# A graph attention layer on one core: groups of 12 tiles for groups of 8, and one-hots turned by a five-row matmul

## The reference

```python
def head(w1, bb1, w2, bb2, a1, aab1, a2, aab2):
    feats = jnp.maximum(x @ w1 + bb1, 0.0) @ w2 + bb2          # (12500, 64)
    x_cat = jnp.concatenate([feats[row], feats[col], elem[:, None]], axis=1)
    hid = jnp.maximum(x_cat @ a1 + aab1, 0.0)                  # (200000, 129)
    e1 = leaky_relu((hid @ a2 + aab2)[:, 0], 0.2)
    w = jnp.exp(e1 - jnp.max(e1))
    pooled = segment_sum(w[:, None] * feats[col], row, n)
    row_sum = segment_sum(w, row, n) + 1e-10
    return pooled / row_sum[:, None]
h = vmap(head)(...)                                            # 4 heads
out = layernorm(x + transpose(h, (1, 0, 2)).reshape(n, -1))
```

## Time and profile before

| | |
|---|---|
| median of 3 runs | 4587.36 us (4585.55 to 4588.11) |
| the profiled execution | 4587.18 us, span 4585.4 us |
| TensorE, busy share of the span | 90% |
| VectorE | 89% |
| ScalarE | 72% |
| GpSimd | 51% |
| tile loop: first to last hidden part | 1316 to 4451 us |

### The profile page before, as it was taken

One profiled execution on the slowest core, in us unless ns is written; L12 is line 12 of the kernel. 1 busy time (PEld: TensorE's weight loads), 2 busy tenths in 40 slices (PEclk: granted clock), 3 DMA queues, 4 the chain that ended last, 5 costly groups with the idle time before them and its releaser, 6 DMA issues.

```text
span 4585.4 us, 128801 instructions
## 1 busy us (share of the span) xinstructions
PE 4132.6 (90%) x25516; PEld 2946.2 (64%) x25517; DVE 4094.2 (89%) x21278; ACT 3319.3 (72%) x11283; POOL 2340.7 (51%) x2495
## 2 busy tenths in 40 slices
PE   2599999999889999999999999999999999999990
PEld 1255555555567777777777777777777777777760
DVE  8888888888779999999999999999999999999988
ACT  1244444444468888888888888888888888888875
POOL 5444444444445555555555555555555555555535
PEclk9799999999989999999999999999999999999995
DMA  2144444444477777777777777777777777777757
GB/s 90 42 99 89 104 96 91 102 96 93 99 220 224 228 223 226 222 224 226 225 224 223 225 227 221 225 225 226 226 220 223 227 226 223 223 226 224 218 157 224
DMA packets 266911, 851.78 MB, mean 186 GB/s; under 512 B 107916, under 2 KB 109584, under 8 KB 266861
## 3 DMA queue, kind: packets, MB, share of 16 engines
q0 software_dynamic: 169920, 673.54, 52.8%
q1 hardware_dynamic: 63543, 160.18, 11.7%
q10 hardware_dynamic: 33398, 17.49, 1.5%
HBM read 739.10 MB, written 111.90 MB: 186 GB/s over the span
## 4 chain that ended last, share of the span: by engine, by line
PE 38%; ACT 28%; issue 3%; DVE 2%; DMA 0%; ACTq 0%; POOL 0%; DVEq 0%; SPq 0%; POOLq 0%
ACT z L1191 19%; PE psum L1003 16%; PE psum L1007 9%; PE psum L990 9%; ACT onehot L1220 4%; ACT onehot_t L1209 3%; PE psum L1016 3%; ACT onehot L1224 2%; PE psum L971 1%; DVE z L1727 1%; DVE z L1720 1%; PE psum L1027 0%; ACT onehot L1222 0%; DVE z L1743 0%; DVE z L1738 0%
## 5 line engine op out<-in xcount | busy, mean ns | idle before, releaser
L761 POOL DMA_INDIRECT z<-qf_table,rec x1664 | 1605.9, 965 | 1458.8 <-PE psum L990 1038.6
L1191 ACT ACTIVATE z<-z 128x64 f32<-128x64 f32 x6656 | 1651.1, 335 | 0.0
L1003 PE MATMUL psum<-p_win,onehot_t 128*128 x9984 | 1409.7, 274 | 87.2 <-ACT onehot_t L1209 67.0
L1003 PEld LDWEIGHTS psum<-p_win,onehot_t 128*128 128x128 bf16 x9984 | 966.5, 97 | 541.6 <-issue 213.0
L990 PE MATMUL psum<-z,onehot 128*128 128x260 f32 x3328 | 1031.9, 392 | 3.8 <-DVE acc L1655 3.5
L1007 PE MATMUL psum<-z,ident 128*128 128x258 f32 x3328 | 1002.2, 383 | 0.0
L1606 DVE SCALAR_TENSOR_TENSOR z<-z,a_b 128x129 f32<-128x129 f32 x3328 | 881.4, 289 | 3.7 <-issue 0.2
L1606 DVE SCALAR_TENSOR_TENSOR z<-psum,a_b 128x129 f32<-128x129 f32 x3328 | 827.5, 286 | 0.0
L721 POOL DMA_INDIRECT sorted_rows<-z x300 | 475.0, 1583 | 635.9 <-DVE z L1484 487.3
L1596 DVE TENSOR_TENSOR z<-z,psum 128x258 f32<-128x258 f32 x1664 | 698.0, 419 | 98.5 <-PE psum L1007 97.2
L1655 DVE TENSOR_TENSOR acc<-acc,psum 125x260 f32 x1664 | 701.5, 422 | 26.2 <-PE psum L990 4.1
(11 more groups left out here) (230 smaller groups left out, 4602.9 us busy)
## 6 DMA issues: line engine op xcount, KB each, us to landing
p_table<-acc SPq DMA_DIRECT2D x100, 338.6 KB
p_win<-p_table SPq DMA_DIRECT2D x100, 338.6 KB
z<-qf_table,rec POOLq DMA_INDIRECT x1664, 4.5
qf_table<-acc SPq DMA_DIRECT2D x75, 339.5 KB
acc<-in_x_dram SPq DMA_DIRECT2D x25, 448.0 KB
z<-in_x_dram SPq DMA_DIRECT2D x20, 560.0 KB
out_dram<-z ACTq DMA_DIRECT2D x20, 560.0 KB
qf_table<-z SPq DMA_DIRECT2D x25, 339.5 KB
```

Source lines behind the costliest of these rows:

```text
L761: pool.indirect_dma_start(out=z_t[:, o + j, :], out_offset=None, in_=qf_table, in_offset=bass.IndirectOffsetOnAxis(ap=rec[:, o + j, 3:4].b ...
L1003: mm = pe.matmul(to, onehot_t[:, j, :], p_flat[:, bass.ds((w % 2) * (3 * ZW) + (part * ZW + o), n)], start=(part == 0), stop=(part == 2 an ...
L1191: op = act.activation(z_t[:, slot, o:o + DO], z_t[:, slot, o:o + DO], ACT.Copy, scale=z_t[:, slot, o + DO:o + HF])
```

## The change

- Groups of 12 tiles (`SB` = 12) in three batches of four, in the same ring of 24 slots, which now holds two groups. The padded number of tiles is 1668, 139 groups.
- `onehot_t` gets 24 slots. Its rows below 125 come from one bf16 matmul for four tiles, of `node_k` (five rows: 2n, -1, -1, and 1-n*n in two parts, for the ramp n) with `edge_k` (five rows: the edge's row r, r*r in two parts, and ones), so that the result is 1-(r-n)^2, and ACT takes it with a Relu. Rows 125 to 127, the parts of the edge's weight, are written by a DMA for a whole group, and so are the first three rows of `edge_k` (`load_edges`, begun a group ahead; both come from a new table `row_feats`).
- `onehot` (edges in partitions) has only 12 slots and is made in the step in which it is used; its rows come from a small load of their own (`load_rows`). Records shrink to two words.
- Sums follow the hidden part by 18 tiles (`LAG` = 6) where it was 16; gathers go to the group ahead as slots come free.
- The record stage writes three tables: ScalarE copies fields, GpSimd squares the rows and splits the squares, SP stores records, rows and features. PE turns three fields and not six.

```diff
-    SB = 8
+    SB = 12
+    BATCH = 4
+    NBATCH = SB // BATCH
+    LAG = 6
     RING = 24
...
-        onehot = sb("onehot", [P, RING, P])
-        onehot_t = sb("onehot_t", [P, SB, P], BF16)
-        rec = sb("rec", [P, RING, 4])
+        onehot = sb("onehot", [P, SB, P])
+        row_e = sb("row_e", [P, RING])
+        onehot_t = sb("onehot_t", [P, RING, P], BF16)
+        rec = sb("rec", [P, RING, 2])
...
@@ PE, turn @@
-                    group = (i * SPB + (k + off)) * 2 + u
-                    pe.wait_ge(s_onehot, group + 1)
-                    since(pe, s_oht, group)
-                    for j in range(HALF_SB):
-                        mm = pe.transpose(psum[:, 6, j * P:(j + 1) * P], onehot[:, ((k + off) * SB + u * HALF_SB + j) % RING, :], ident[:, :])
-                    mm.then_inc(s_oht_mm, 1)
+                    batch, kn = (i * SPB + (k + off)) * NBATCH + u, (k + off) % SPB
+                    if u == 0:
+                        pe.wait_ge(s_edge_k[kn], i * 16 + ((k + off) // SPB + 1) * 16)
+                    since(pe, s_oht, batch)
+                    pe.matmul(psum[0:WN, 6, 0:BATCH * P], node_k[:, 0:WN], edge_k[:, kn, u * BATCH:(u + 1) * BATCH, :].rearrange("p t n -> p (t n)"),
+                              start=True, stop=True).then_inc(s_oht_mm, 1)
...
@@ PE, step @@
-                    if j == SB // 4 and live(i, k, 0):
+                    if j == 0 and live(i, k, 0):
                         turn(0, 1)
...
+                    if j == 4 and live(i, k, 0):
+                        turn(0, 2)
+                    if j == 8 and live(i, k, 1):
                         turn(1, 0)
...
-                    if j < SB - 1 and live(i, k, -2):
-                        sum_up(-2, j)
+                    if j < LAG and live(i, k, -2):
+                        sum_up(-2, j + SB - LAG)
+                    if j >= LAG and live(i, k, -1):
+                        sum_up(-1, j - LAG)
...
@@ ACT @@
+                def load_rows():
+                    kn = k % SPB
+                    act.dma_start(row_e[:, kn * SB:(kn + 1) * SB], edge_rows[:, bass.ds((i * SPB + k) * SB, SB)]).then_inc(s_row_e[kn], 16)
+
+                def load_edges():
+                    kn = (k + 1) % SPB
+                    if live(i, k, -1):
+                        act.wait_ge(s_z_mm, tile(-1, SB - 1) + 2)
+                    act.dma_start(onehot_t[WN:P, kn * SB:(kn + 1) * SB, :],
+                                  row_feats[bass.ds((i * SPB + (k + 1)) * SB, SB), 3:6, :].rearrange("t f n -> f t n")).then_inc(s_edge_w[kn], 16)
+                    act.dma_start(edge_k[0:3, kn, :, :], row_feats[bass.ds((i * SPB + (k + 1)) * SB, SB), 0:3, :].rearrange("t f n -> f t n"))\
+                       .then_inc(s_edge_k[kn], 16)
+
+                if live(i, k, -1):
+                    onehots(0)
+                if live(i, k, 1):
+                    load_edges()
                 if live(i, k, 0):
                     take_turned(0, 1)
-                if live(i, k, 1):
-                    onehots(1, 0)
                 if live(i, k, -1):
                     exps()
-                if live(i, k, 2):
+                if live(i, k, 0):
+                    load_rows()
+                if live(i, k, 1):
                     load_records()
                 for j in range(SB):
                     if live(i, k, -1):
                         weight(j)
-                    if j == 0 and live(i, k, 1):
+                    if j == 3 and live(i, k, -1):
+                        onehots(1)
+                    if j == 4 and live(i, k, 0):
+                        take_turned(0, 2)
+                    if j == 7 and live(i, k, 1):
                         take_turned(1, 0)
-                    if j == SB // 2 and live(i, k, 1):
-                        onehots(1, 1)
+                    if j == 9 and live(i, k, -1):
+                        onehots(2)
```

More of the change, by code:

```diff
@@ L373, in gnn_layer @@
         CR = 5
-        SC = next(NSB // n for n in range(1, NSB) if NSB % n == 0 and NSB // n <= P)
-        KS = NSB // SC
+        SC = next(NSH // n for n in range(1, NSH) if NSH % n == 0 and NSH // n <= P)
+        KS = NSH // SC
         assert CGROUPS * CG == W and CGROUPS % CR == 0
@@ L413, in gnn_layer @@
         N_PARTS = 5
-        N_TAB_STEPS = 13
+        N_TAB_STEPS = 14
+        assert SB == 12 and all(t * 683 >> 13 == t // SB for t in range(NT))
         EMPTY_W = CHUNKS // P * SF
@@ L419, in gnn_layer @@
         N_PICK = EC // CH
[L420 to L421 removed]
+        BULK = NTS // P
         def live(i, k, off):
@@ L694, in _ @@
             pool.wait_ge(s_weights, N_W)
[L695 to L701, removed]
@@ L967, in _ @@
                 pe.wait_ge(s_stage[g % 4], g // 4 * 16 + 16)
-                since(pe, s_field_a, g - 1)
-                since(pe, s_field_b, g - 1)
-                for f in range(NF):
-                    mm = pe.matmul(psum[:, g % 2 * 6 + f // 3, f % 3 * P:(f % 3 + 1) * P],
+                since(pe, s_field_a, 2 * g - 2)
+                for f in range(3):
+                    mm = pe.matmul(psum[:, g % 2 * 6, f * P:(f + 1) * P],
                                    stage[:, g % 4, :].rearrange("p (s f) -> p f s", f=NF)[:, f, :], ident[:, :], start=True, stop=True)
@@ L1203, in take_turned @@
                 def take_turned(off, u):
[L1205 to L1220 removed]
+                    batch, at = (i * SPB + (k + off)) * NBATCH + u, (k + off) % SPB * SB + u * BATCH
@@ new lines, in take_turned, with onehots @@
+                    if live(i, k, off - 2):
+                        act.wait_ge(s_z_mm, tile(off - 2, u * BATCH + BATCH - 1) + 2)
+                    act.wait_ge(s_oht_mm, batch + 1)
+                    act.activation(onehot_t[0:WN, at:at + BATCH, :].rearrange("p t n -> p (t n)"), psum[0:WN, 6, 0:BATCH * P], ACT.Relu).then_inc(s_oht, 1)
+                def onehots(u):
+                    batch, own, kn = (i * SPB + (k - 1)) * NBATCH + u, slice(u * BATCH, (u + 1) * BATCH), (k - 1) % SPB
+                    if u == 0:
+                        act.wait_ge(s_row_e[kn], i * 16 + ((k - 1) // SPB + 1) * 16)
+                    if live(i, k, -2):
+                        act.wait_ge(s_agg, tile(-2, u * BATCH + BATCH - 1) + 1)
+                    for j in range(u * BATCH, (u + 1) * BATCH):
+                        op = act.activation(onehot[:, j, :], iota_row[:, :], ACT.Abs, scale=-1.0, bias=row_e[:, kn * SB + j:kn * SB + j + 1])
@@ L1221, in onehots @@
                     op.then_inc(s_row_dist, 1)
-                    act.activation(onehot[:, oo:oo + HALF_SB, WN:P], rec_b[:, oo:oo + HALF_SB, 2:5], ACT.Copy)
-                    act.wait_ge(s_row_dist, group + 1)
-                    act.activation(onehot[:, oo:oo + HALF_SB, 0:WN], onehot[:, oo:oo + HALF_SB, 0:WN], ACT.Relu, scale=-1.0,
-                                   bias=ones_f[:, 0:1]).then_inc(s_onehot, 1)
+                    act.wait_ge(s_row_dist, batch + 1)
+                    act.activation(onehot[:, own, :], onehot[:, own, :], ACT.Relu, scale=-1.0, bias=ones_f[:, 0:1]).then_inc(s_onehot, 1)
```

272 lines of the change are left out of this document (163 added, 109 removed).

## The result

| | before | after |
|---|---|---|
| median | 4587.4 us (4 runs) | 4969.4 us (4 runs, 4952.6 to 4986.8) |
| ratio, 95% interval | | 1.0834 (1.0795 to 1.0872) |
| the profiled execution | 4587.18 us | 4952.55 us, span 4950.8 us |
| first hidden part of the loop | 1316.4 us | 1312.7 us |
| first matmul of the last stage | 4473.2 us | 4838.4 us |

The change makes the kernel 8.3% slower. The forecast was 4618 us, within 4490 to 4690. The direction was right; the size was not, and the time is outside the range.

What follows compares the result with a forecast made beforehand. A ring of waits through ScalarE's in-order queue was taken as the bound; 4587 us plus 23 (139 groups of 22.75 us against 208 of 15.09), 3 for the record stage and 5 for the drain gave 4618 us, range 4490 to 4690.

Steps and rivals of the forecast that it cites:

- The ring: Chain of waits through ScalarE's in-order queue and TensorE's tile 8, claimed to set a 12-tile group at 22.75 us.
- register loop: Engines going round their loop at the group start, with TensorE starting cold: 0.3 us, an estimate without a row.
- `e_sh` to first scaling: On ScalarE, two exponentials and two exposed DMA issues between `e_sh`'s start and the first scaling: 1.37 us.
- `e_sh` to tile 8: From `e_sh`'s start through ScalarE's scalings, a one-hot batch and the take to TensorE's tile 8: 9.08 us.
- tile 8 to next tile 0: On TensorE, four tiles of 1.535 us and a turn of 0.22: 6.36 us.
- tile 0 to the transpose of maxima: On TensorE, from the next group's tile 0 to its transpose of the maxima: 4.39 us.
- transpose to `e_sh`: From the transpose of the maxima to the start of `e_sh`, which VectorE makes: 2.62 us.
- the turn: TensorE's five-row bf16 matmul of 512 columns replacing four fp32 transposes: 0.22 us, upper bound 0.43.
- rival 3: TensorE's clock halves after the new 2.5 us gap: 4683 us for a quarter of groups, 4891 for all; chance 0.16.
- Rivals 1: ScalarE's DMA issues run before `e_sh` comes, so a group takes 21.88 us: 4497 us in all; chance 0.15.
- Rival 2: No ring in the tile loop, the fullest engine binds: 20.5 us a group, 4306 us in all; chance 0.12.
- Outside the loop: Record stage, 3 us more, and the drain's extra scalings and batches, 5 us more.

Runs made afterwards that it cites:

- experiment 8: Changed kernel with tile 8's wait filled by nine unused products and the turn on 128 rows of constants (one-hots wrong): 4661.9 us, ratio 1.0162 to the kernel before.
- experiment 2: Changed kernel with nine unused 128-column fp32 products on TensorE ahead of tile 8's wait: 4745.9 us, ratio 1.0343 to the kernel before.
- experiment 3: Changed kernel with the DMA issue of the rows' load moved ahead of the exponentials: 4766.9 us, ratio 1.0385 to the kernel before.
- experiment 1: Changed kernel with the third turned batch's take ahead of the second one-hot batch and tile 4's scalings: 4442.5 us, ratio 0.9686 to the kernel before.
- 10: Kernel of experiment 1 with the turn over all 128 rows, right data, nothing left out: 4378.1 us, ratio 0.9544 to the kernel before.

## Why the prediction came out wrong

**The ring was right.** The take on ScalarE behind scalings and a batch of one-hots sets tile 8, TensorE idles there, and the group is no shorter for being rebuilt. Its terms at full clock, the measured ones as means of 20 groups without and 18 with a turn of the register loop:

| from | forecast | measured, no loop turn | measured, with one |
|---|---|---|---|
| `e_sh` to first scaling | 1.37 | 1.37 | 1.37 |
| `e_sh` to tile 8 | 9.08 | 9.11 | 9.11 |
| tile 8 to next tile 0 | 6.36 | 6.91 | 7.46 |
| tile 0 to the transpose of maxima | 4.39 | 4.83 | 4.82 |
| transpose to `e_sh` | 2.62 | 2.49 | 2.60 |
| register loop | 0.3 | 0 | in the terms above |
| sum | 22.75 | 23.33 | 23.99 |

The register loop comes round in every second group, so the mean is 23.66 us (23.64 over the 45 groups), and the loop's share of it, 0.33 us, was forecast well.

**First mis-sized term: the turn, 0.22 for 0.55 us.** I took it from columns alone and gave it an upper bound of 0.43, the price of the four transposes, both of which have 128 rows. There are two in the ring: 0.66 us of the 0.89 us between 22.75 and 23.64, and experiment 8 takes 0.60 of it back. The rest is 0.1 us each at tiles 8 and 0, whose first hidden part takes 0.92 us and not 0.82, another 0.12 ahead of tile 0, and 0.13 less behind the transpose of the maxima. The bound was too low, and the trace of before held a better row than the one I used. It spreads the maxima with a matmul of four rows:

```profile
2705.98 0.60 PE L1007 MATMUL psum<-z,ident 128*128 128x258 f32 x2
2706.51 0.38 PE L1027 MATMUL psum<-max_diag,ones_f 4*128 4x4 f32 x2
2706.82 0.71 PE L990 MATMUL psum<-z,onehot 128*128 128x260 f32 x2
```

It has four columns and still takes 0.31 us, and 0.53 us pass from the fp32 pair to it where 0.43 pass to a sum. The nearest row was the one with few rows, not the one that did the same job. The whole 0.89 us makes 139 x 0.89 = 124 us. By itself it would have put the forecast at 4742 us, past the range; experiment 2, the ring without falls, measures 4746. The sign was the ring's doing and not luck, for the kernel is 3.4% slower even at full clock.

**Second: the clock, named as rival 3 and given 0.16.** This is the larger part, 139 x 1.53 = 212 us. The step that failed is the reading of the earlier trace rows, that TensorE stayed at 2.4 GHz after an idle of 1.97 us at 109.94. The trace's record of the clock begins only at 114.24 us, and a window before that is shown as 1.00 for want of a record. The pace of the transposes tells the clock there. Below are those behind that idle, then the ones of the turn in a window whose clock is 0.50, and the same in the loop, at 1.00 (ns, shortest, median and longest, then the first and last start):

```profile
L813 PE MATMUL psum<-ident,z x16: 421/421/455, 109.9 to 113.2; 128*100 128x128 f32 x16
...
1314.00:1316.00 2.00, 1.12 (x4) 0.50 0.62 130
L1016 PE MATMUL psum<-ident,onehot x4: 421/421/476, 1314.3 to 1315.0; 128*128 128x128 f32 x4
...
L1016 PE MATMUL psum<-ident,onehot x4: 273/273/273, 2712.3 to 2712.6; 128*128 128x128 f32 x4
```

At 109.94 one takes 421 ns and they start 0.213 us apart, both as at half clock; at 1.00 they start 0.109 apart. So TensorE was at 1.2 GHz there, and no row spoke against a fall behind an idle of 2 us. The other row spoke for one: before the fall near 4455 TensorE had only idled for 0.85 and 0.74 us. In the changed kernel 81 of 126 idles of some 2.05 us have a fall beside them. Rival 3's two times are also 5 us low by its own terms (4618 + 70 = 4688 and 4618 + 278 = 4896). The price of a fall, 2 us, was near: 1.40 us for the short stretch and 2.83 for the long one, 2.37 in the mean of the 81. The rival's upper case, 4891 us with a fall in every group, is near the measured 4952.6 only because the ring was longer; in truth two thirds of the groups had one. The Trainium skill ("TensorE: Matmul & The Clock Gate", section "HAM oscillation — how this bites in real kernels") describes kernels whose matmuls come in bursts with waits between, and which then spend part of their time at the lower level. By that the changed kernel should show both levels inside one group, and the trace agrees: 468 us at half clock between 1500 and 4700.

**Rivals 1 and 2 fall.** The first issue starts 0.06 us after the second exponential does (2607.60, 2607.66) and the scaling only 0.05 us behind the second issue; experiment 3 moves one of them and finds its 0.52 us. Rival 2 wanted TensorE not to wait at tile 8; it waits there in all 127 groups. With the take moved, experiment 1, the rival's case becomes true, though at 21.47 us and not at 20.5: again the turns, three of them at 0.55.

**Outside the loop** I took 8 us. The loop starts 3.7 us earlier, for the shorter record stage, and filling and draining it take 9.4 us more (3525.7 us from the first hidden part to the last stage, less 139 x 25.17, against 3156.7 less 3139): 5.7 us in all.

Against the forecast of 4618 us, the ring adds 124, the clock 212 and this takes 2 off: 4952 us, where the profiled execution took 4952.55. Since filling and draining are what is left over beside 139 mean groups, this is a split of the measured time and not a test of it; the test is in experiments 1, 2, 8 and 10. The other runs of this kernel, up to 4986.8 us, had a mean clock of 0.914 to 0.924 where the profiled one had 0.922. The one with 0.924 took 4965.8 us, so the clock alone doesn't put them in order, and what makes them differ is not shown.

## What to carry to other kernels

A wait of TensorE has two prices, its own length and what the clock takes after it; price both, and where the second matters and the wait can't be moved, work that nobody needs may be cheaper than idling. In an in-order queue ask of each consumer-facing step what stands ahead of it: the whole difference between 8% slower and 3% faster was one instruction that stood behind a batch and four scalings and not ahead of them. Before a row is taken as evidence of the clock, see that the record of the clock covers it, and test it by the pace of a known instruction. Bound an unseen matmul by a row of its own row count, not by the operation that it replaces, and where they are fewer than its neighbours', try it padded to the same number.

## What the hardware showed unexpectedly

- Among matmuls of 128 rows, one of 5 or of 64 rows and 512 columns lengthened its tile by 0.55 us, one of 128 rows by 0.22 us. The Trainium skill ("TensorE: Matmul & The Clock Gate", section "LDWEIGHTS (loading the stationary operand)") says that the time of a weight load follows from columns and not from rows. The load itself agrees, 0.13 us against 0.14; what differs is when it may start, and on that the measurement decides.
- Idles of 1.5 to 2.1 us, one in some 24 us of nearly unbroken work, were enough for half clock beside half to two thirds of them. The same idle of 2.12 us went with a fall in one group (2710.95) and with none in another (2616.32), and groups without falls came several in a row. So the length isn't all that decides, and what else does was not tried.
